# Local attention in units of four heads by 128 keys, with stacked 64-query blocks and values moved inside SBUF

## The reference

```python
q = l2norm(q) * qs
k = l2norm(k) * ksc
q, k = rotary_xpos(q, k)
...
bk, bv = (look_around(bk), look_around(bv))
sim = jnp.einsum('bhwid,bhwjd->bhwij', bq, bk)
mask = (i < j) | (i > j + WINDOW) | (j == -1)
sim = jnp.where(mask, -jnp.finfo(sim.dtype).max, sim)
attn = jax.nn.softmax(sim, axis=-1)
out = jnp.einsum('bhwij,bhwjd->bhwid', attn, bv)
...
x = x + o @ wo
```

## Time and profile before

| | us |
|---|---|
| median of 3 runs | 2269.81 (2269.67 to 2273.56) |
| the profiled execution, its own time | 2267.61 |
| its span, first to last instruction | 2265.8 |
| TensorE busy over the span | 1887.1 (83%) |
| VectorE busy | 1730.5 (76%) |
| ScalarE busy | 1326.7 (59%) |
| first scores of layer 0 | 1325.2 |
| last second-half scores of layer 1 | 2145.7 |

### The profile page before, as it was taken

How to read it: one execution, slowest core, us unless ns; L and a number is a source line. 1 busy time by engine, 2 the same in 40 slices (tenths; PEclk the granted TensorE clock), 3 DMA queues, 4 the chain that set the end, 5 groups by cost and what they waited for, 6 DMA issues and landing times. The chain is left out here.

```text
span 2265.8 us, 38842 instructions
## 1 busy us (share of the span) xinstructions
PE 1887.1 (83%) x12576; PEld 1040.6 (46%) x12576; DVE 1730.5 (76%) x4306; ACT 1326.7 (59%) x2865; POOL 840.5 (37%) x703
## 2 busy tenths in 40 slices
PE   6888888875898988769717579999999999999985
PEld 2333333332444444434315346666656566666543
DVE  6999999994677777412166679999986899999875
ACT  5777777731444444324252368888873688888731
POOL 5777777751022222224421433333321333333211
PEclk8999999995999999879958889999999999999997
DMA  5333333203011111023171400000001000000011
GB/s 152 116 100 113 109 115 117 89 29 99 23 36 43 39 37 43 23 82 109 45 210 51 132 24 6 6 1 1 2 4 26 1 6 6 1 1 1 4 35 29
DMA packets 102297, 117.06 MB, mean 52 GB/s; under 512 B 27780, under 2 KB 78255, under 8 KB 101104
## 3 DMA queue, kind: packets, MB, share of 16 engines
q1 hardware_dynamic: 98000, 106.51, 16.1%
q0 software_dynamic: 4096, 8.06, 1.1%
HBM read 71.44 MB, written 38.11 MB: 48 GB/s over the span
## 5 line engine op out<-in xcount | busy, mean ns | idle before, releaser
L392 POOL TENSOR_TENSOR m_bu<-m_dtu,m_brow 128x1024 f32<-128x1024 f32 x128 | 300.4, 2360 | 58.8 <-DVE m_hs L807 57.0
L807 DVE TENSOR_TENSOR_SCAN m_hs<-m_ps_da,m_bu 128x1024 f32<-128x1024 f32 x128 | 291.9, 2281 | 3.6 <-POOL m_bu L392 2.5
L1355 ACT ACTIVATE a_pt<-a_ps_s 128x1024 f32<-128x1024 f32 x128 | 131.1, 1025 | 227.5 <-PE a_ps_s L1133 227.5
L2851 ACT ACTIVATE l_pe<-l_ps_s,l_nbias,l_qs 128x192 f32<-128x192 f32 (+1 forms) x512 | 244.8, 487 | 32.3 <-DVE l_nbias L3007 32.3
L513 PE MATMUL m_ps_y_ps<-m_prod,m_ident 128*128 128x512 f32 x512 | 248.4, 608 | 0.0
L1472 DVE TENSOR_REDUCE a_mpad<-a_ps_s 128x4 f32<-128x1024 f32 x128 | 156.8, 1225 | 93.7 <-PE a_ps_s L1125 92.7
L1125 PE MATMUL a_ps_s<-a_heads 32*128 32x256 f32 x1024 | 187.9, 447 | 44.3 <-DVE a_mpad L1472 28.5
L659 ACT ACTIVATE m_ps_da<-m_dt,m_a_neg 128x510 f32<-128x510 f32 x256 | 166.0, 681 | 72.2 <-DVE m_hs L807 71.9
L1133 PE MATMUL a_ps_s<-a_qm,a_heads 32*128 32x256 f32 x1024 | 184.7, 437 | 1.8 <-ACT a_pt L1355 1.4
L2623 PE MATMUL l_ps_s<-l_kT,l_qT 128*128 128x384 f32 (+1 forms) x512 | 179.9, 433 | 0.0
L2861 ACT COPY l_pT<-l_ps_t 128x256 f32<-128x256 f32 (+1 forms) x256 | 122.9, 480 | 72.5 <-PE l_ps_t L2633 45.8
(11 more groups left out here) (336 smaller groups left out, 4454.6 us busy)
## 6 DMA issues: line engine op xcount, KB each, us to landing
m_brow<-state_rows SPq DMA_DIRECT2D x64, 512.0 KB, 4.3
slots<-m_void SPq DMA_DIRECT2D x16, 516.0 KB, 5.4
e_xs<-slots SPq DMA_DIRECT2D x16, 258.0 KB, 2.7
ys<-m_void SPq DMA_DIRECT2D x8, 512.0 KB, 5.4
qk<-a_qk SPq DMA_DIRECT2D x16, 256.0 KB, 2.0
a_heads<-qk SPq DMA_DIRECT2D x64, 64.0 KB
ew_w<-in_w SPq DMA_DIRECT2D x2, 2048.0 KB, 11.6
e_yy<-ys SPq DMA_DIRECT2D x16, 256.0 KB, 5.4
```

The source lines that it names most:

```text
L392: nc.gpsimd.tensor_tensor(bu[s % 4][:, :, :], dtu[p][:, :, :], b2, ALU.mult).then_inc(bu_rd, 1)
L807: dve.tensor_tensor_scan(hs[s % 4][:, :, :].rearrange("p h t -> p (h t)"), da[s % 2][:, :, :, :].rearrange("p h q t -> p (h q t)"), bu[s % ...
L2851: nc.scalar.activation(pe_[u % 2][:, h, 0:nk], s_ps[u % 2][:, h * 192:h * 192 + nk], ACT.Exp, bias=nbias[:, u % 2, h:h + 1], scale=qs[b % ...
```

## The change

A unit now has four heads (HU = 4) and always 128 keys, so a block has 4 units instead of 8, two for each half. A second-half unit handles its two blocks of 64 queries apart: block r of 64 queries meets exactly the 128 keys from 64 before its start, as a matmul with 64 rows of output, and the two are stacked in the 128 partitions of the bank. The mask has 4 x 128 columns for each half. `divide` becomes one `tensor_tensor` over four heads with a broadcast reciprocal; `transpose_p` has always four transposes. In `weigh`, second-half units multiply the 64 queries of r = 1 by the values of tokens 128 to 255, and those of r = 0 by `near`, values of tokens 64 to 191, which two DMAs on SP (`bring_near`) copy from `v` inside SBUF. `v` has three buffers instead of four, `hT` two instead of one.

The order of each engine's `attend` is rewritten for four units. On TensorE `scores(u)` is now followed by `transpose_p(u - 1)`, and `weigh(u - 2)` stands later in the same step; on VectorE `maxima(u)` is followed by a `square_sums` and `divide(u - 1)`. The projections are spread over the four units anew. The diff, cut (of the three `attend` the old lines are left out, they stand above):

```diff
-    U, Q, K = NCH * NP, 0, 1
+    HU, Q, K = 4, 0, 1
+    NU = NH // HU
+    U = NCH * NU
...
+        v = [m.sb(f"v{i}", [P, NCH, INNER]) for i in range(3)]
+        near = [m.sb(f"near{i}", [P, INNER]) for i in range(2)]
+        top, nbias = m.sb("top", [P, HU]), m.sb("nbias", [P, 2, HU])
+        pe_ = [m.sb(f"pe{i}", [P, HU, P]) for i in range(2)]
+        rs, ri = m.sb("rs", [P, 2, HU]), m.sb("ri", [P, HU])
+        pn = [m.sb(f"pn{i}", [P, HU, P]) for i in range(2)]
+        pT = [m.sb(f"pT{i}", [P, HU, P]) for i in range(2)]
...
+                def bring_near(n, b):
+
+                    l, z, k = at[n], b % 3, NB * n + b
+                    sp.wait_ge(l.v_sb, NCH * (b + 1))
+                    at_least(sp, l.pv_mm, U * (b - 1))
+                    if n == 1 and b < 2:
+                        sp.wait_ge(at[0].pv_mm, U * (NB - 1 + b))
+                    at_least(sp, near_in, 32 * k)
+                    sp.dma_start(near[k % 2][0:HD, :], v[z][HD:P, 0, :]).then_inc(near_in, 16)
+                    sp.dma_start(near[k % 2][HD:P, :], v[z][0:HD, 1, :]).then_inc(near_in, 16)
...
-                for g in range(NG):
-                    gather(0, g)
-                for g in range(3):
-                    gather(1, g)
+                for n in range(2):
+                    for b in range(NB):
+                        bring_near(n, b)
+                        if b in (3, 5):
+                            gather(n, b // 2 - 1)
+                    for g in range(2, NG if n == 0 else 3):
+                        gather(n, g)
...
                 def scores(n, b, u):
-                    l, p, c, j = at[n], b % 2, u // NP, u % NP
+
+                    l, p, c, d = at[n], b % 2, u // NU, u % NU
                     i = U * b + u
-                    if j == 0:
+                    if d == 0:
                         pe.wait_ge(l.xT_sb[Q], NCH * b + c + 1)
                         pe.wait_ge(l.xT_sb[K], 2 * (NCH * b + c + 1))
-                    at_least(pe, l.ex_rd, 2 * (i - 1))
-                    k0 = 0 if c == 0 else P - HD
-                    nk = P if c == 0 else 192
-                    both = s_ps[u % 2][:, 0:384].rearrange("p (h k) -> p h k", h=2)[:, :, 0:nk]
-                    pe.matmul(both, identb[:, :], mask[:, :, 192 - nk:], start=True, stop=False)
-                    pe.matmul(both, qT[p][:, j, c * P:(c + 1) * P], kT[p][:, :, j, k0:k0 + nk],
-                              start=False, stop=True).then_inc(l.s_mm, 1)
+                    at_least(pe, l.ex_rd, HU * (i - 1))
+                    bank = s_ps[u % 2][:, :].rearrange("p (h k) -> p h k", h=HU)
+                    pe.matmul(bank, identb[:, :], mask[:, c, :, :], start=True, stop=False, skip_group_check=True)
+                    for k in range(2):
+                        j = 2 * d + k
+                        if c == 0:
+                            last = pe.matmul(bank[:, 2 * k:2 * k + 2, :], qT[p][:, j, 0:P], kT[p][:, :, j, 0:P],
+                                             start=False, stop=True, skip_group_check=True)
+                        else:
+                            for r in range(2):
+                                q0 = P + r * HD
+                                last = pe.matmul(bank[r * HD:(r + 1) * HD, 2 * k:2 * k + 2, :], qT[p][:, j, q0:q0 + HD],
+                                                 kT[p][:, :, j, q0 - HD:q0 + HD], start=False, stop=True, skip_group_check=True)
+                    last.then_inc(l.s_mm, 1)
 
                 def transpose_p(n, b, u):
 
-                    l, c = at[n], u // NP
+                    l = at[n]
                     i = U * b + u
                     pe.wait_ge(l.pn_rd, i + 1)
                     at_least(pe, l.pT_sb, i - 1)
-                    for h in range(2):
-                        last = pe.transpose(t_ps[u % 2][:, h * P:(h + 1) * P], pn[u % 2][:, h, P:2 * P], ident[:, :])
-                    if c == 1:
-                        for h in range(2):
-                            last = pe.transpose(t_ps[u % 2][:, (2 + h) * P:(3 + h) * P], pn[u % 2][:, h, 0:P], ident[:, :])
+                    for h in range(HU):
+                        last = pe.transpose(t_ps[u % 2][:, h * P:(h + 1) * P], pn[u % 2][:, h, :], ident[:, :])
                     last.then_inc(l.pT_mm, 1)
 
                 def weigh(n, b, u):
-                    l, z, c, j = at[n], b % 4, u // NP, u % NP
+                    l, z, c, d = at[n], b % 3, u // NU, u % NU
                     pe.wait_ge(l.pT_sb, U * b + u + 1)
-                    if j == 0:
+                    if d == 0:
                         at_least(pe, l.oT_sb, NCH * b + c)
                         if c == 0:
                             pe.wait_ge(l.v_sb, NCH * (b + 1))
                             if b == 0 and n == 1:
                                 pe.wait_ge(ff[0].ob_rd, NG)
-                    for h in range(2):
-                        dst = o_ps[h * HD:(h + 1) * HD, j * P:(j + 1) * P]
-                        cols = slice((2 * j + h) * HD, (2 * j + h + 1) * HD)
-                        last = pe.matmul(dst, v[z][:, c, cols], pT[u % 2][:, h, :], start=True, stop=(c == 0), skip_group_check=True)
-                        if c == 1:
-                            last = pe.matmul(dst, v[z][:, 0, cols], pT[u % 2][:, 2 + h, :], start=False, stop=True, skip_group_check=True)
+                        else:
+                            k = NB * n + b
+                            pe.wait_ge(near_in, 32 * (k + 1))
+                    for k in range(2):
+                        j = 2 * d + k
+                        if c == 0:
+                            for h in range(2):
+                                cols = slice((2 * j + h) * HD, (2 * j + h + 1) * HD)
+                                last = pe.matmul(o_ps[h * HD:(h + 1) * HD, j * P:(j + 1) * P], v[z][:, 0, cols], pT[u % 2][:, 2 * k + h, :],
+                                                 start=True, stop=True, skip_group_check=True)
+                        else:
+                            for r in range(2):
+                                vals = near[(NB * n + b) % 2][:, :] if r == 0 else v[z][:, 1, :]
+                                for h in range(2):
+                                    cols = slice((2 * j + h) * HD, (2 * j + h + 1) * HD)
+                                    dst = o_ps[h * HD:(h + 1) * HD, j * P + r * HD:j * P + (r + 1) * HD]
+                                    last = pe.matmul(dst, vals[:, cols], pT[u % 2][:, 2 * k + h, r * HD:(r + 1) * HD],
+                                                     start=True, stop=True, skip_group_check=True)
                     last.then_inc(l.pv_mm, 1)
...
                 def attend(n, b, first=False, last=0):
...
                     l = at[n]
+                    scores(n, b, 0)
+                    if not first:
+                        transpose_p(n, b - 1, U - 1)
+                    if last < 2:
+                        project(n, b + 1, 0, Q)
+                    if not first:
+                        weigh(n, b - 1, U - 2)
+                        if last < 2:
+                            pe.wait_ge(l.v_sb, NCH * (b + 1))
+                        else:
+                            pe.wait_ge(l.res_rd, NCH * (b - 1))
+                        output(n, b - 1, 0)
+
+                    scores(n, b, 1)
+                    transpose_p(n, b, 0)
+                    turn_k(n, b, 1)
+                    if not first:
+                        weigh(n, b - 1, U - 1)
+                    if last < 2:
+                        turn_q(n, b + 1, 0)
+                        if not first:
+                            pe.wait_ge(l.res_rd, NCH * (b - 1) + 1)
+                        project_v(n, b + 1, 0)
+                        project(n, b + 1, 0, K)
+
+                    scores(n, b, 2)
+                    transpose_p(n, b, 1)
+                    if last < 2:
+                        project(n, b + 1, 1, Q)
+                    weigh(n, b, 0)
+                    if not first:
+                        if last < 2:
                             pe.wait_ge(l.v_sb, NCH * (b + 1) + 1)
+                        else:
+                            pe.wait_ge(l.res_rd, NCH * (b - 1) + 1)
+                        output(n, b - 1, 1)
+                    if last < 1:
+                        if first:
+                            pe.wait_ge(l.v_sb, NCH * (b + 1) + 1)
+                        else:
+                            pe.wait_ge(l.res_rd, NCH * b)
+                        transpose_r(n, b + 2)
+
+                    scores(n, b, 3)
+                    transpose_p(n, b, 2)
+                    if last < 2:
+                        turn_k(n, b + 1, 0)
+                    weigh(n, b, 1)
+                    if last < 2:
+                        turn_q(n, b + 1, 1)
+                        if last == 0:
+                            pe.wait_ge(l.hT_sb, 2 * (b + 3))
+                        else:
```

(136 more changed lines are left out.)

124 lines of the change are left out of this document (21 added, 103 removed).

## The result

The changed kernel takes 2646.36 us (median of 4 runs, 2641.57 to 2652.91) against 2269.74 us of the kernel before: a ratio of 1.165, 95% interval 1.163 to 1.168. The forecast was 2625 in a range of 2505 to 2745. The profiled execution has a span of 2646.0 us.

The account below looks back on a forecast made before the run. The prediction took the chain of TensorE and VectorE waiting for each other in turn as the bound. From 2267.6 us, the chain adds 287 and clock falls 72, giving 2626.6, taken as 2625, range 2505 to 2745.

Parts of the forecast that it names:

- The mechanism: Local attention: transposes directly behind scores wait for VectorE's division, projections stand behind them, and VectorE waits for those.
- the walk: Sum of slots and hand-overs along one steady local-attention block, from the start of one K projection: 32.95 us against 23.46.
- The chain: Scores, maximum, division, transposes, projections in turn: 32.95 us a block against 23.46, +287 us over both layers.
- Second-half weighing: Eight 64-column matmuls a unit on TensorE: between 0.6 (columns bind) and 1.2 us (instructions bind), taken as 0.9.
- VectorE's terms: Slots on the walk, among them maximum and bias 0.81, squares 0.60, residual and key scaling 0.98 us.
- The clock: TensorE falls to half clock after every second gap: 2 a block at 1.5 us, 0.8 on the chain, +72 us.
- The clock holds: Rival: the clock stays as it is now in this phase, 2267.6 + 287 = 2555 us; chance 0.20.
- The clock stays low: Rival: low clock over most of the phase, 11 us a block added, 2885 us; chance 0.08.
- 64-row matmuls one after the other: Rival: 64-row pairs don't run side by side in second-half scores and weighing, +57 us, 2680 us; chance 0.08.
- The bound stays TensorE's busy time: Rival: the division's wait is covered, a block takes about 20.2 us, total 2171 us; chance 0.07.
- Edits at nothing: SBUF copies, larger mask table, extra memset and doubled hT: no cost beyond 0 to 1.5 us and 0.1 once.
- The tiling rule: Mode changes drain TensorE: two more on the chain a block at 0.17 us each, 10 us higher, inside the range.

Follow-up runs that it names:

- filled kernel: Changed kernel with eight more bf16 matmuls of 512 columns ahead of each TensorE wait for the division: 2547.8 us, ratio 1.105.
- squares-last: Changed kernel with VectorE's reduction of squares moved from before the division to behind it, in all four stages: 2531 us, ratio 1.098.
- repaired order: Changed kernel, transposes two units behind scores, residual and key scaling earlier on VectorE: ratio 0.969; with K projections also ahead of V, 0.961 and 20.66 us a block.

## Why the prediction was right

**The mechanism** was the walk's: transposes that wait for the division of their own stage, projections behind them, VectorE waiting for those. The waits are where it put them, and undoing that one step of the order takes the loss away.

**The chain** was sized at 32.95 us a block and is 31.49 at full clock. Most of what was too large is TensorE's. Second-half weighing, taken as 0.9 between 0.6 and 1.2, measures 0.61 to 0.62 (columns bind, not the number of instructions); in the filled kernel, with the turned queries behind it:

```profile
1614.33 0.34 PE L2690 MATMUL l_ps_o<-l_pT,l_near 128*64 128x64 f32 x4
...
1614.72 0.29 PE L2690 MATMUL l_ps_o<-l_pT,l_v 128*64 128x64 f32 x4
1614.94 0.66 PE L2619 MATMUL l_ps_qk<-t_ident,l_c 128*128 128x128 f32 x4
```

Behind a wait four transposes are followed by a projection after 0.49, not 0.59, which then reaches its reader in 1.06, not 1.16; turned keys and queries take 0.53 and 0.49, not 0.60 each. First half to the next K projection: 15.14 against 16.12; second half 16.36 against 16.83. VectorE's terms held but for one: the 512-element maximum takes 0.68, the division 0.70, residual and key scaling 0.80 where the walk had 0.98. For both layers the walk said +287, the filled kernel's stage says 2 x (497.2 - 372.6) = +249.

**The clock** was the term that was too small: 2.4 us a block, +72, from two falls a block at 1.5 with 0.8 of each on the chain. Measured: 35.4 - 31.5 = 3.9 us a block; 2 x (557.8 - 497.2) = +121 by the stages, 127 by the times of the two programs and 136 by their ratios. The price of one fall, taken from the earlier trace rows, held: a block with two falls takes 34.4 us, 2.9 over the 31.5 of the filled kernel, and the one fall of squares-last costs 1.6. Two other factors were too small. Nearly all of a fall is on the chain, not 0.8 of it; and there are 2.7 falls a block, not 2, since in some blocks the clock falls after all four gaps. 2.7 falls at 1.5 are 4.0, near the 3.9. The two errors, -38 of the chain and +49 or more of the clock, nearly cancel. That 2625 is so close to 2646 is in this part luck.

**The rivals.** The clock holds: no (0.86), though the filled kernel shows what it would have been, 249 us over the kernel before where the rival had 287. The clock stays low: no, it costs 3.9 us a block where the rival had 11. 64-row matmuls one after the other: no. The bound stays TensorE's busy time: not in this kernel, but it is what the repaired order reaches, at 20.7 us a block against the rival's 20.2. **Edits at nothing:** the copies stay at nothing in blocks of equal clock.

**The tiling rule** of the Trainium skill that the prediction weighed ("TensorEngine Tiling (Array Packing)", Key Properties: changing the mode drains TensorE) fits the rows in kind: from the bias matmul to the first 64-row score it is 0.31 us, to the first 128-row score at the same place 0.22, and to the transposes 1.32 against 1.08. A second-half unit thus pays 0.24, of which the way back and the pairs themselves weren't told apart. The prediction weighed two changes at 0.17, 0.34 a block; the rows give 0.5 a block of TensorE's time.

**What stays open:** how the surplus of the old units under the new order (+544 against 380) divides beyond the estimate above, what decides after which gap the clock falls, and how much of the final 3.9% is the larger units' and how much the better order's.

## What to carry to other kernels

Count, for each instruction that waits on another engine, how many units stand between the request and the work it needs; where an engine asks for something of the very stage in which its partner is held up by it, busy shares say nothing of the time, and the sum of the chain does. Larger units need the same distance as small ones: here they came out 3.9% faster in the old distance, with the awaited steps and K ahead, and cost 16.5% at one unit less. A stall of TensorE was paid twice here, as idle time (8.0 us a block) and as half clock on the work behind it (3.9); useless matmuls in the gaps show the second part by themselves.

## What the runs showed of the hardware that I had not expected

Idle gaps of 2.4 to 3.3 us, four in 35 us, held the granted clock at a mean of 0.86, between its levels of 1.2 and 2.4 GHz, with TensorE busy two thirds of the time; filling 1.7 us of each gap with matmuls that nobody reads brought 1.00 and 127 us or more. With squares behind the division and gaps unfilled, each some 0.6 us shorter, the mean was 0.95. Each fall made a block of these two kernels 1.5 to 1.6 us longer. That idle gaps of TensorE lose the clock is also what the Trainium skill says (page "TensorE: Matmul & The Clock Gate", Why this matters for your kernels). The runs agree in kind, but the page speaks of longer gaps: here the clock fell after one of 2.25 us in the earlier trace rows and one of 2.41 us in the block above.

An fp32 matmul of 64 rows and 64 columns costs what its columns cost when pairs fill the array: 16 records take 0.61 us, and 8 records of 128 columns take 0.59.
